# A fused attention and mixture-of-experts layer: TensorE's queue in the expert-tile loop without three repeated waits and two register copies, and expert numbers packed three to a word

## The reference, cut to what matters

```python
x = x + attention(layernorm(x))            # x: 4096 tokens of 256; 16 heads of 16, causal window of 64
xf = layernorm(x)
scores = sigmoid(xf @ gate_w.T + lb_bias)  # 8 experts
topw, topi = top_k(scores, 2);  topw = topw / (topw.sum(-1) + 1e-8)
out = 0
for e in range(8):
    m = topi == e
    wmean = (topw * m).sum() / max(m.sum(), 1)
    y = (silu(xf @ gate[e].T) * (xf @ up[e].T)) @ down[e].T     # 256 -> 128 -> 256
    out = out + where(m.any(-1), y * wmean, 0)
x = x + out + shared_mlp(xf)               # the same form, 256 -> 256 -> 256
```

## Time and profile before

| what | us |
|---|---|
| median of 3 runs | 559.91 |
| lowest, highest | 557.99, 563.6 |
| profiled execution, own time | 565.39 |
| its span, first to last instruction | 563.6 |
| first attention work to the last row of the sweep and the routing table | up to about 384 |
| tile loop | about 384 to 508 |
| shared expert's remaining units, output | about 508 to 564 |

### The profile page before, as it was taken

The page is one execution under the profiler, slowest core; times in us unless marked ns, Lnnn a source line. Parts: engine busy times, 40 slices in busy tenths (PEclk is TensorE's granted clock), DMA queues, the critical chain, the costliest instruction groups (busy, mean ns, idle before and its releaser), DMA issues.

```text
span 563.6 us, 16371 instructions
## 1 busy us (share of the span) xinstructions
PE 522.6 (93%) x5529; PEld 419.1 (74%) x5529; DVE 387.1 (69%) x1194; ACT 339.2 (60%) x776; POOL 228.4 (41%) x419
## 2 busy tenths in 40 slices
PE   7799999899999899999998868889999999999997
PEld 4567877776776776776677546778888888788996
DVE  6566688778788778788776656765666665563665
ACT  4577787776786777777685623224666766662111
POOL 5100112335244245245333336731555555454651
PEclk9899999989999999999998987979999999999999
DMA  6260101312321321320210123678555554435994
GB/s 209 67 200 5 41 4 42 98 29 94 98 67 55 108 66 46 109 89 33 72 60 33 70 80 116 229 228 254 160 153 157 149 160 147 135 107 174 397 400 170
DMA packets 42559, 69.16 MB, mean 123 GB/s; under 512 B 9708, under 2 KB 28655, under 8 KB 42480
## 3 DMA queue, kind: packets, MB, share of 16 engines
q1 hardware_dynamic: 33984, 43.46, 24.5%
q0 software_dynamic: 6480, 17.31, 8.7%
q10 hardware_dynamic: 2016, 7.34, 3.8%
HBM read 36.43 MB, written 32.06 MB: 122 GB/s over the span
## 4 chain that ended last, share of the span: by engine, by line
PE 87%; DVE 5%; issue 3%; ACT 3%; another core or an unknown queue 1%; POOL 0%; DVEq 0%; ACTq 0%; POOLq 0%
PE ps L569 41%; PE ps L628 9%; PE ps L658 6%; PE ps L821 5%; PE ps L912 4%; PE ps L623 4%; PE ps L639 3%; PE ps L644 3%; PE ps L667 3%; PE ps L580 2%; PE ps L673 2%; PE ps L929 2%; PE ps L705 1%; PE ps L781 1%
## 5 line engine op out<-in xcount | busy, mean ns | idle before, releaser
L513 POOL DMA_INDIRECT z_slots<-z,slot x64 | 64.7, 1011 | 121.6 <-PE ps L628 101.3
L569 PE MATMUL ps<-wF,wA 128*128 x639 | 104.9, 303 | 1.4 <-issue 0.6
L554 POOL DMA_INDIRECT y_rows<-vm,dest x71 | 69.5, 979 | 69.3 <-issue 44.4
L569 PEld LDWEIGHTS ps<-wF,wA 128*128 128x128 f32 x639 | 84.8, 188 | 13.7 <-issue 5.8
L1225 DVE TRANSPOSE_TENSOR_REDUCE rmax<-ps 128x32 f32<-128x1024 f32 x64 | 79.6, 1244 | 17.2 <-PE ps L628 15.7
L1016 ACT ACTIVATE probs<-ps 128x1024 f32<-128x1024 f32 x64 | 65.6, 1026 | 33.8 <-PE ps L644 33.0
L628 PE MATMUL ps<-bd,kT 64*128 64x256 f32 x512 | 68.8, 390 | 0.0
L569 PE MATMUL ps<-yT,wA 128*128 128x256 f32 x384 | 62.0, 299 | 1.5 <-DVE yT L1198 1.5
L628 PEld LDWEIGHTS ps<-bd,kT 64*128 64x128 f32 x512 | 51.8, 199 | 5.8
L569 PEld LDWEIGHTS ps<-yT,wA 128*128 128x128 f32 x384 | 50.1, 192 | 4.7 <-issue 2.0
L1123 ACT ACTIVATE vt<-ps 128x256 f32<-128x256 f32 x32 | 12.2, 384 | 58.2 <-PE ps L569 56.4
(11 more groups left out here) (202 smaller groups left out, 1147.7 us busy)
## 6 DMA issues: line engine op xcount, KB each, us to landing
z<-z_slots SPq DMA_DIRECT2D x71, 136.0 KB
zT_scratch<-zT SPq DMA_DIRECT2D x16, 512.0 KB
bd<-y_rows SPq DMA_DIRECT2D x8, 512.0 KB, 9.6
out<-xs SPq DMA_DIRECT2D x16, 256.0 KB, 7.7
wraw_of<-wffn SPq DMA_DIRECT2D x10, 384.0 KB
xs<-x SPq DMA_DIRECT2D x7, 512.0 KB, 4.0
wA<-zT_scratch ACTq DMA_DIRECT2D x7, 512.0 KB, 6.3
z<-y_rows SPq DMA_DIRECT2D x4, 512.0 KB, 9.9
```

The costliest lines, as they stand in the source:

```text
L513: eng.indirect_dma_start(z_slots, bass.IndirectOffsetOnAxis(ap=slot[:, c, j, t:t + 1], axis=0), z[:, c, t, :], None, bounds_check=E * REGI ...
L554: eng.indirect_dma_start(y_rows, bass.IndirectOffsetOnAxis(ap=dest[:, m:m + 1], axis=0), yo[:, m, :], None, bounds_check=K * T - 1, oob_is ...
L569: mm = eng.matmul(out, lhsT(a), rhs(b), start=start and n == 0, stop=stop and n == 2, skip_group_check=skip)
```

## The change

Three things are done to PE's queue in the tile loop. First, `rows_T`, `tile_gate_up` and `hidden_T` lose the wait `after(eng, ..., t - 1)`: each repeats what an earlier wait of the same queue has already seen. Second, `expert_of` with its register copy at every use goes (two a tile), and so does the copying of the loaded words (`donate=True`); each tile has a register of its own. Third, a word holds three experts' numbers instead of eight, in the same 3 bits each. The number is masked in place and not shifted down: it stands in the register as e, 8e or 64e, and the address factor 768 is divided by 1, 8 or 64 instead. The table becomes 24 words instead of 9, and the step that finds the expert stands inside `tile_gate_up` of the tile before, ahead of its third matmul.

```diff
-    return -(-expert_tiles(T) // 8)
+    return -(-expert_tiles(T) // PACK)          # PACK = 3
...
-                def product(out, lhsT, rhs, start, stop, skip=False):
+                def product(out, lhsT, rhs, start, stop, skip=False, ahead=None):
                     for n, (a, b) in enumerate(((0, 0), (0, 1), (1, 0))):
+                        if n == 2 and ahead:
+                            ahead()
...
                     eng.load(pack_regs, tile_packs[0:1, :])
                     for r in pack_regs:
-                        packs.append(eng.snap(r, min_val=0, max_val=8 ** 8 - 1))
-                expert_regs = [eng.alloc_register(f"expert_{m}") for m in range(4)]
+                        packs.append(eng.snap(r, donate=True, min_val=0, max_val=E ** PACK - 1))
+                experts = {}
                 def find_expert(t):
-                    eng.reg_mov(expert_regs[t % 4], (packs[t // 8] >> (3 * (t % 8))) & (E - 1))
-                def expert_of(t):
-                    return eng.snap(expert_regs[t % 4], min_val=0, max_val=E - 1)
+                    unit = E ** (t % PACK)
+                    r = eng.alloc_register(f"expert_{t}")
+                    eng.reg_mov(r, packs[t // PACK] & ((E - 1) * unit))
+                    experts[t] = eng.snap(r, donate=True, min_val=0, max_val=(E - 1) * unit) * (6 * P // unit)
...
-                def weights(e, a, c0, c1):
-                    return wF[a][:, bass.ds(e, 1), c0:c1].rearrange("p o c -> p (o c)")
+                def weights(at, a, c0, c1):
+                    return wF[a][:, :, :].rearrange("p e c -> p (e c)")[:, bass.ds(at + c0, c1 - c0)]
                 def rows_T(t, q, m):
                     eng.wait_ge(s_zin[m], 16 * (q + 1))
-                    after(eng, s_zl, t - 1)
...
                 def tile_gate_up(t, q, m):
-                    e = expert_of(t)
+                    e = experts[t]
                     eng.wait_ge(s_zl, t + 1)
-                    after(eng, s_h1, t - 1)
                     for k in range(KT):
                         mm = product(ps[:, m % 2, 0:2 * P], lambda a: z1[:, m % 2, a, k * P:(k + 1) * P],
-                                     lambda b: weights(e, b, 2 * k * P, 2 * (k + 1) * P), k == 0, k == KT - 1)
+                                     lambda b: weights(e, b, 2 * k * P, 2 * (k + 1) * P), k == 0, k == KT - 1,
+                                     ahead=(lambda: find_expert(t + 1)) if k == 0 and t + 1 < NTS else None)
...
                 def hidden_T(t, q, m):
                     eng.wait_ge(s_h1, t + 1)
-                    after(eng, s_hTl, t - 1)
...
                 def tile_down(t, q, m):
-                    e = expert_of(t)
+                    e = experts.pop(t)
```

More of the change, by code:

```diff
@@ L39 @@
 K = 2
+PACK = 3
 ZR = D + 16
@@ L56, in constants @@
     for name, n in (("token", T // P), ("before", P), ("region", E), ("expert", E), ("lower", E * E),
-                    ("upto", E * E), ("tile_rows", T // P), ("tile", expert_tiles(T)), ("choice", K), ("quad", HPT // 2), ("index", 1), ("octal", 8 * expert_packs(T))):
+                    ("upto", E * E), ("tile_rows", T // P), ("tile", expert_tiles(T)), ("choice", K), ("quad", HPT // 2), ("index", 1), ("octal", PACK * expert_packs(T))):
         at[name] = (c, n)
@@ L143, in layer @@
         NPK = expert_packs(T)
-        tile_digits, tile_packs = sb("tile_digits", [P, 8 * NPK]), sb("tile_packs", [P, NPK], I32)
+        tile_digits, tile_packs = sb("tile_digits", [P, PACK * NPK]), sb("tile_packs", [P, NPK], I32)
         tile_sums = sb("tile_sums", [P, NPK])
@@ L947, in tile @@
                         tile_down(*later(q, m, -1))
-                    if 8 * q + m + 2 < NTS:
-                        find_expert(8 * q + m + 2)
                 sweep(eng, step, prologue, epilogue)
@@ L955, in _ @@
                 find_expert(0)
-                find_expert(1)
                 eng.wait_ge(s_hf, NS * GA)
@@ L1473, in tile_places @@
                     chain(eng.tensor_tensor(tile_digits[:, :], tile_digits[:, :], const("octal"), ALU.mult))
-                    chain(eng.tensor_reduce(tile_sums[:, :], tile_digits[:, :].rearrange("p (n j) -> p n j", j=8), AX.X, ALU.add))
+                    chain(eng.tensor_reduce(tile_sums[:, :], tile_digits[:, :].rearrange("p (n j) -> p n j", j=PACK), AX.X, ALU.add))
                     chain(eng.tensor_copy(tile_packs[:, :], tile_sums[:, :]))
@@ L1652 @@
         "index": p[:, None],
-        "octal": 8 ** (np.arange(8 * expert_packs(T)) % 8),
+        "octal": E ** (np.arange(PACK * expert_packs(T)) % PACK),
     }
```

## The result

The changed kernel takes **570.14 us** (median of 4 runs, 566.67 to 573.4) against 561.75 for the kernel before (4 runs, 557.99 to 564.39): a ratio of 1.014, 95% interval 1.010 to 1.019. The forecast was 543.1. On another chip the sign turned over: the same changed kernel, unedited, gave 0.9745 (0.971 to 0.978) there (e9). Executions over 1.5% slower than the fastest of the same kernel are left out of every ratio (one of e2's, which is the profiled one, and two of e3's), so a ratio need not be that of the medians.

The account below looks back on a forecast made before the run. PE's queue was taken as the bound, 1.66 to 1.70 us a tile against the array's 1.40. The loop's -18.1 us and the longer table's +1.3 gave -16.8, from the median 559.91 to 543.1 us, range 537 to 553.

Parts of the forecast that it names:

- What bounds the kernel: Tile loop: PE's queue hands out a tile's work in 1.66 to 1.70 us; the array could do it in 1.40.
- The three waits and the copies: PE's queue in the tile loop: three waits save 0.34 us a tile, two moves and 0.9 operations 0.33.
- The array is late next: Tile loop: with the queue relieved the array sets the period, 1.43 us for 1.70, 18.1 us less over 67 periods.
- The mask inside `tile_gate_up`: Between second and third matmul: can make the array wait 0.1 us without queue lead; counted within 0.03 a tile.
- My upper end of 1.50: Tile loop: the longest period allowed for in the forecast case, leaving a gain of 13.4 us.
- The longer table: Before the loop: PE's load of 24 words costs 1.5 us more; with the copy gone +1.3, from -0.2 to +2.2.
- The sum: Whole kernel: -18.1 us from the loop and +1.3 from the load give -16.8 us, 543.1 us against the median.
- that hop: Tile loop, `tile_down` through ACT to DVE's low part: 0.12 us left; as another engine's bound, 551.1 us, chance 0.12.
- That the removed instructions cost little: Rival, PE's queue in the loop: only 0.08 us a tile gained, 555.8 us (554 to 558); chance 0.08.
- The slower rival: Loop's head: the 24-word load and one more half-clock stretch cost 5.4 us, the loop gives nothing: 565.3 us; chance 0.03.
- My sign for being wrong: Tile loop: a period staying above 1.6 us would mean the queue's 0.1 us wasn't an instruction's cost.
- The other sign: Tile loop: PE waiting for DVE L1559 or ACT L1176 tile after tile would also show the forecast wrong.

Follow-up runs that it names:

- e9: The changed kernel, unedited, on a third chip where the kernel before takes 533.85 us: 520.06 us, ratio 0.9745.
- e2: The changed kernel with two extra masks a tile on TensorE's queue (13 control instructions), first chip: 566.78 us, ratio 1.011.
- e3: The kernel before with only the three repeated waits taken out (12 control instructions a tile), first chip: 566.54 us, ratio 1.006.
- e1: The changed kernel with three extra masks a tile on TensorE's queue (15 control instructions), first chip: 562.32 us, ratio 1.003.
- e13: The kernel before with only the three repeated waits taken out, on a chip where the kernel before takes 533.93 us: 513.84 us, ratio 0.963.
- e14: The changed kernel with the three waits put back, on a chip where the kernel before takes 533.93 us: 519.43 us, ratio 0.974.
- e7: The changed kernel with three extra masks a tile plus a semaphore increment on each matmul that had none, second chip: 534.31 us, ratio 1.002.
- e5: The changed kernel without the third product in a tile's gate-up and down (9 matmuls for 12), second chip: 508.3 us, ratio 0.953.
- e4: The changed kernel with the three waits put back (12 control instructions a tile), first chip: 566.74 us, ratio 1.012.
- e6: The changed kernel with the third product of gate-up and down 32 columns wide instead of 256, second chip: 514.56 us, ratio 0.963.

## Why the prediction was wrong

**What bounds the kernel.** Right. The queue hands out a tile's work in 1.64 us with 15 control instructions, 1.48 with 13, and with 12 or 9 the array's 1.40 is what is left. Instructions of another kind at the same count (e1) give the same period, so it is their number that costs. From 15 to 13 it is 0.08 us each, a little less than the 0.1145 I took.

**The three waits and the copies.** Right in mechanism, but the sum wasn't carried to its end: by my own price 12 instructions need 12 x 0.1145 = 1.37 us, already under the array's 1.40, so one half was enough. The three waits alone take the queue to the array's floor (e13, 1.41); the packing and the copies had nothing left to give, and with the waits put back into the changed kernel its period hardly moves (e14, (461.0 - 357.6) / 70 = 1.48 for 1.47).

**"The array is late next", 1.43.** This is the step that failed. On the first chip the array is late next only in the undisturbed tile, 1.40. What is late after that is TensorE's semaphores, which I had no term for: 31 of the 70 periods are over 1.8 us, up to 3.5, and the mean is 1.79. 70 x (1.79 - 1.43) = 25 us are the miss of 27. The sign was in the trace of before: 5 silu late by 4.4 us together in the loop, one by 1.6 us, and the waits for L639 in the attention, up to 1.4:

```profile
DVE negm L1230 <- PE ps L639: 27.6, 35, 1.4
```

In a kernel paced by its queue they cost little, and I read them as noise. On chips without this, the step held with 1.47 for 1.43.

**The mask inside `tile_gate_up`.** I counted it within 0.03; it costs 0.05 and was the larger part of what separates 1.47 from 1.41. My upper end of 1.50 held it.

**The longer table.** Right in size: +1.5 for the load was forecast, 1.3 and 1.07 measured. With the copy's 0.18 gone the path should have grown by 1.3; the pause grew by 0.6 on the first chip and by 0.8 from e13 to e9. By the Trainium skill's 200 ns a register cited there ("Runtime: NRT & Kernel Launch", Instruction fetch mechanics) the load would have grown by 3.4, an estimate that neither kind of chip bears out.

**The sum.** -16.8 us of 565.39, a ratio of 0.970, was forecast. Where nothing is late: 520.06 - 533.85 = -13.8 us, 0.9745. By its parts: 70 x (1.69 - 1.47) = 15.4 less the load's 1.1 (1.69 is e7's period, on the kind of chip of e9, at the pace of the kernel before).

**The rivals.** None was it. On the first chip TensorE does wait for DVE's low part in the loop, 9 times and 4.6 us together, but behind late semaphores and not tile after tile; in e9 and e13 it never does, so 1.41 to 1.47 us a tile leaves that hop enough time. POOL becomes the bound only at 1.29 (e5). That the removed instructions cost little is refuted where nothing is late: the three waits alone take the period from 1.69 (e7, at the pace of the kernel before) to 1.41 (e13). The slower rival named the head of the loop and one more stretch at half clock; the pause grew by 0.6 us (2.56 to 3.14), the loop starts 0.3 us later, and the slowing was elsewhere. My sign for being wrong, a period above 1.6, did come, but its reading ("the queue's 0.1 us wasn't the cost of an instruction") would have been false: the mean hid tiles of 1.40 and of 2.5. The other sign was the right one in kind, since ACT and DVE do wait now, but for TensorE.

**Open.** What holds back TensorE's semaphores on the first kind of chip. Shown is that it becomes frequent with pace (e1 against e2 to e4), that several of them are held back together, that DVE's semaphores are on time in the stretch shown, that long waits for TensorE also stand in the attention, and that the granted clock is 1.00 in the loop while it happens. Whether it counts matmuls, columns or tiles wasn't settled: e5, e6 and their repeats were made for that, and all fell on chips that don't have it. Nor is it known whether it belongs to the chip or to its moment, as no chip was measured at two times.

## What to carry to other kernels

Look at the distribution of a loop's periods, not at the mean alone: a mean of 1.79 made of 1.40 and 2.5 is another illness than a steady 1.79. When an engine's queue is relieved, the slack that it gave to everything that waits for it goes too, so a rare long wait for that engine in the trace of before deserves a term of its own in the sum. Put address arithmetic behind a group of matmuls and not between two of them, try the halves of a change one by one (here one half gave all), and repeat on a second chip before believing a few per cent of either sign.

## What was not expected of the hardware

- One program, two times: the kernel before takes 561 us in the first result and in e1 to e4, and 533.7 to 533.9 on each of the four chips after. The mean granted clock of an execution was 0.97 to 0.99 in the slower and 0.98 to 1.00 in the faster, and in the changed kernel VectorE's longest wait for one and the same transpose was 2.3 and 0.6 us.
- On the first chip TensorE's semaphore came 1.7 us after the matmul's recorded end in the stretch shown, and five came within 0.2 us, with the granted clock at 1.00. On the other chips no silu started over 0.1 us after the recorded end of its gate-up.
- Making the third product of each group 32 columns wide for 256 takes 0.06 us from the tile (1.47 in e9, 1.41 in e6), while leaving it out takes 0.18 (1.29, where POOL binds).
- A TENSOR_LOAD of 24 words took 2.19 us where one of nine took 1.13. A line through these two points is 0.07 us a word on top of 0.5.
